# One more round between the attention and the MLP transposes of the first layer, on every engine

## The chip, the cores and the metric

The kernel runs on one core of one Trainium2 chip, as one launch. The metric is the device time of that core in microseconds (us). A core has five engines that run their own instruction lists in order and meet only at semaphores: PE (TensorE, matmuls and transposes), DVE (VectorE), ACT (ScalarE), POOL (GpSimd) and SP (SyncE, which issues the DMAs). An instruction whose semaphore is not there yet holds up everything behind it on its own engine.

## The reference

The model has four layers of attention and feed-forward on `x` of 16 x 256 x 128 floats. Each half layer is `x = x + layernorm(f(layernorm(x)))`. The change touches the first layer only:

```
def _L0_attn_ref(inputs, Wq, Wk, Wvdown, Wvup):
    Q = inputs @ Wq
    K = inputs @ Wk
    score = jnp.einsum('bqd,bkd->bqk', Q, K) / jnp.sqrt(jnp.float32(D))
    score = jnp.where(causal, score, 0.0)
    score = jnp.where(score != 0, score, NEG_FILL)
    attn = jax.nn.softmax(score, axis=-1)
    V = inputs @ (Wvdown @ Wvup)
    return attn @ V
x = x + _layernorm(_L0_attn_ref(_layernorm(x, axis=-1), ...), axis=-1)
x = x + _layernorm(_L0_ffn_ref(_layernorm(x, axis=-1), ...), axis=-1)
```

`_L0_ffn_ref` is a gated MLP with 384 hidden columns: `silu(x @ wg.T) * (x @ wu.T)`, and then the product with the down weights. The second layer (`L1`) has local and linear attention with an MLP, four times over.

## The kernel before

**Lanes and rounds.** The 4096 rows of `x` are eight groups of 512, each a tile of 128 x 4 x 128. The first phase (`phase1`) takes each group through the first layer (`pe_l0`, `dve_l0`, `act_l0`, `pool_l0`) and the four blocks of the second (`pe_l1` and so on). Four lanes, 0 to 3, take two groups one after the other: lane 0 groups 0 and 4, lane 1 groups 1 and 5. Each engine's list is written by the same scheme: for each lane a generator, and `together` (L140) asks each live lane once a round, lane 0 first, for what it issues up to its next `yield`. A lane joins at the round that `START1 = (0, 4, 9, 13)` (L21) gives. Rounds exist only in the order of the lists; no clock and no barrier belongs to them. A `yield` with nothing ahead of it issues nothing: it moves all that follows in this lane behind the next round of the other lanes.

**The 13 rounds of the first layer.** On PE, step 0 is empty; 1 transposes of the attention input (`pe_tr4`, L289); 2 q, k and v (L667, L668, L672); 3 scores (L681); 4 transposes of the probabilities (L690); 5 probabilities times v (L701); 6 empty; 7 transposes of the MLP input (L289 again); 8 to 10 gate and up (L714, L716), one hidden tile a round; 11 down (L723); 12 empty. A block of the second layer has 17 rounds, the fourth 18. In its order stand transposes (step 2), q and k (3; L743, L744), the values with the first `pe_by_query` (4; L750, L584, L587, L371), the second `pe_by_query` (5), the transposes of the maxima (6; L613), and later `pe_mlp` (L315 up, L324 down).

**What lies between steps 5 and 7.** DVE scales the attention output (L893), takes the statistics (L239, L242), POOL takes the power -1/2 (L276), DVE normalises (L251), adds to `x` (L283), takes the statistics again and negates the mean (L258); POOL takes the power and the product for the shift (L276, L270); ACT normalises in four instructions (`act_norm`, L263), and only then can PE transpose. ACT copies the transposed tile out of PSUM (L297) for step 8.

**What else orders the work.** Lanes 0 and 2 share PSUM banks 4 and 5, lanes 1 and 3 banks 6 and 7 (`lanes1`), and all share banks 0 to 3 for scores and `pe_by_query`. `Banks.fill` makes PE wait, before it fills a bank, for whoever reads what was filled in it last. In step 3 of the first layer DVE masks the scores in eight instructions (L880 to L886), ACT takes the exponentials (L982); silu is L998, the gelu of the second layer's MLP L334. A change among exp, silu and gelu on ACT costs an ACT_TABLE_LOAD.

The phases behind the first (`sync_all(..., "p1")`) begin when all engines are done with it, and the change does not touch them.

Of the kernel before, what the change touches and what calls it, by code (L numbers as in the profile page):

```python
# [160 lines left out]
def build(nc, tables, wa, wb, wc, wd, wm, wi, ve, co, step, frame, xin, out):  # L161
    ctx = ExitStack()
    with ctx:
# [175 lines left out]
        def idle(n):  # L339
            for _ in range(n):  # L340
                yield
# [314 lines left out]
        def pe_l0(pe, c, g):  # L656
            v = views01(c)
            XN, XT, QT, KT = v["XN"], v["XT"], v["QT"], v["KT"]
            k = (g, "l0a")
            yield  # L660
            pe.wait_ge(c.A, (k, "normed", 3))
            pe_tr4(pe, c, k, XN, 0, c.A)
            yield
            pe.wait_dma(got_wa0)
            ps, p2 = c.bank(pe, 0, c.D, (k, "q")), c.bank(pe, 1, c.A, (k, "k"))
            pe.wait_ge(c.A, (k, "xT"))
            pe.e.matmul(ps[0:32, :], wv("wq0"), XT, start=True, stop=True).then_inc(*c.P.inc((k, "q_pe")))  # L667
            pe.e.matmul(p2[0:32, :], wv("wk0"), XT, start=True, stop=True).then_inc(*c.P.inc((k, "k_pe")))  # L668
            pe.wait_ge(AD[LANES], "wv")
            c.banks.fill(pe, 3, c.A, (k, "v"))  # L670
            for t in range(4):
                ins = pe.e.matmul(psum[3][:, t * 128:(t + 1) * 128], XT[:, t * 128:(t + 1) * 128], WV, start=True, stop=True)  # L672
            ins.then_inc(*c.P.inc((k, "v_pe")))
            yield
            pe.wait_ge(c.D, (k, "q"))
            pe.wait_ge(c.A, (k, "k"))
            for b in range(2):
                for n in range(2):
                    t = 2 * b + 1 - n
                    c.banks.fill(pe, 2 * b + n, c.D, (k, b, "masked"))  # L680
                    ins = pe.e.matmul(psum[2 * b + n][:, 0:256], QT[0:32, t * 128:(t + 1) * 128],  # L681
                                      KT[0:32, b * 256:(b + 1) * 256], start=True, stop=True)
                ins.then_inc(*c.P.inc((k, b, "scores")))
            yield
            for b in range(2):
                for n in range(2):
                    c.banks.fill(pe, 2 * b + n, c.A, (k, b, "pT"))
                    pe.wait_ge(c.A, (k, b, n, "exp"))
                    for j in range(2):
                        ins = pe.e.transpose(psum[2 * b + n][:, j * 128:(j + 1) * 128],  # L690
                                             v["sc"][:, b, n, j * 128:(j + 1) * 128], ident)
                ins.then_inc(*c.P.inc((k, b, "tr")))
            yield
            ps = c.bank(pe, 0, c.D, (k, "o"))
            pe.wait_ge(c.A, (k, "v"))
            for b in range(2):
                pe.wait_ge(c.A, (k, b, "pT"))
                for n in (1, 0):
                    t = 2 * b + 1 - n
                    for j in range(2):  # L700
                        ins = pe.e.matmul(ps[:, t * 128:(t + 1) * 128], v["sT"][:, b, n, j * 128:(j + 1) * 128],  # L701
                                          v["V0"][:, 2 * b + j, :], start=j == 0, stop=j == 1)
            ins.then_inc(*c.P.inc((k, "av")))
            yield
            k = (g, "l0f")
            yield
            pe.wait_ge(c.A, (k, "normed", 3))
            pe_tr4(pe, c, k, XN, 0, c.A)
            yield
            pe.wait_ge(DD[LANES], "wgu")  # L710
            for j in range(3):
                ps, p2 = c.bank(pe, 0, c.A, (k, "h", j)), c.bank(pe, 1, c.D, (k, "hu", j))
                pe.wait_ge(c.A, (k, "xT"))
                pe.e.matmul(ps[:, :], WGU[:, j * 128:(j + 1) * 128], XT, start=True, stop=True).then_inc(  # L714
                    *c.P.inc((k, "gate", j)))
                pe.e.matmul(p2[:, :], WGU[:, 384 + j * 128:384 + (j + 1) * 128], XT, start=True, stop=True).then_inc(  # L716
                    *c.P.inc((k, "up", j)))
                yield
            ps = c.bank(pe, 0, c.A, (k, "y"))
            pe.wait_ge(c.D, (k, "hu", 2))  # L720
            for t in range(4):
                for j in range(3):
                    ins = pe.e.matmul(ps[:, t * 128:(t + 1) * 128], v["h3"][:, j, t * 128:(t + 1) * 128], wgd[:, j, :],  # L723
                                      start=j == 0, stop=j == 2)
            ins.then_inc(*c.P.inc((k, "sum")))
            yield
            yield
# [134 lines left out]
        def dve_l0(dve, c, g):  # L862
            v = views01(c)
            X, XN, O4, Z, VQ = XG[g], v["XN"], v["O4"], v["Z"], v["VQ"]
            k = (g, "l0a")
            dve.wait_dma(got_x[g])
            dve_stats(dve, c, k, X)
            yield
            yield
            dve.wait_ge(c.P, (k, "q_pe"))  # L870
            dve.e.tensor_scalar(v["QT"][0:32, :], c.ps[0][0:32, :], float(32.0 ** -0.5), None, ALU.mult).then_inc(
                *c.D.inc((k, "q")))
            yield
            dve.wait_dma(got_step)
            st, step2 = v["st"], bass.AP(tensor=STEPM.tensor, offset=STEPM.offset, ap=[STEPM.ap[0], [128, 2], [1, 256]])
            for b in range(2):
                src = PS[:, 1024 * b:1024 * b + 1024].rearrange("p (n c) -> p n c", c=512)[:, :, 0:256]
                sc, zz = v["sc"][:, b, :, :], v["zz"][:, b, :, :]
                dve.wait_ge(c.P, (k, b, "scores"))
                dve.e.tensor_tensor(sc, src, step2, ALU.mult).then_inc(*c.D.inc((k, b, "masked")))  # L880
                dve.wait_ge(c.D)
                dve.e.tensor_scalar(zz, sc, 0.0, FMIN, ALU.is_equal, ALU.mult).then_inc(*c.D.inc())
                dve.wait_ge(c.D)
                dve.e.tensor_tensor(sc, sc, zz, ALU.add).then_inc(*c.D.inc())
                dve.wait_ge(c.D)
                dve.e.tensor_reduce(st[:, 2 * b:2 * b + 2], sc, X_AX, ALU.max, negate=True).then_inc(*c.D.inc((k, b, "max")))  # L886
            yield
            yield
            dve.wait_ge(c.A, (k, 1, 0, "exp"))
            dve.e.reciprocal(st[:, 8:12], st[:, 4:8]).then_inc(*c.D.inc())  # L890
            dve.wait_ge(c.D)
            dve.wait_ge(c.P, (k, "av"))
            dve.e.tensor_tensor(O4, v4(c.ps[0]), st[:, 8:12].unsqueeze(2).to_broadcast([128, 4, 128]), ALU.mult).then_inc(  # L893
                *c.D.inc((k, "o")))
            yield from dve_post(dve, c, (g, "l0ap"), X, O4)
            k = (g, "l0f")
            dve_stats(dve, c, k, X)
            yield
            yield
            for j in range(3):  # L900
                dve.wait_ge(c.A, (k, "h", j))
                dve.wait_ge(c.P, (k, "up", j))
                dve.e.tensor_tensor(v["h3"][:, j, :], v["h3"][:, j, :], c.ps[1][:, :], ALU.mult).then_inc(
                    *c.D.inc((k, "hu", j)))
                yield
            dve.wait_ge(c.A, (k, "y"))
            yield from dve_post(dve, c, (g, "l0fp"), X, O4)
            yield from dve_norm(dve, c, (g, "z"), X, Z)
            dve.e.memset(VQ[:, :, 64:65], 1.0).then_inc(*c.D.inc((g, "ones")))
# [56 lines left out]
        def act_l0(act, c, g):  # L966
# [24 lines left out]
            k = (g, "l0f")  # L991
            yield
            act_norm(act, c, k, XG[g], v["XN"])
            act_copy(act, c, k, XT, c.ps[0][:, :], "tr", "xT")
            yield
            for j in range(3):
# [58 lines left out]
        def pool_l0(pool, c, g):  # L1055
            v = views01(c)
            yield from pool_norm_shift(pool, c, (g, "l0a"))
            yield from idle(4)
            yield from pool_norm(pool, c, (g, "l0ap"))
            yield from pool_norm_shift(pool, c, (g, "l0f"))  # L1060
            yield from idle(4)
            yield from pool_norm(pool, c, (g, "l0fp"))
            yield from pool_norm(pool, c, (g, "z"))
            pool.e.memset(v["VH"], 0.0).then_inc(*c.G.inc())
            pool.wait_ge(c.G)
            pool.e.memset(v["VP"][:, :, :, 16:17], 1.0)
            pool.e.memset(v["LT"][:, :, 0:64], 0.0)
            pool.e.memset(v["CP"], 0.0).then_inc(*c.G.inc((g // 4, "zeros", c.n)))
# [1720 lines left out]
```

## Time and profile before

| what | value |
|---|---|
| median of the runs | 3525.3 us (3525.18, 3525.3, 3534.24) |
| profiled execution | 3526.35 us |
| its span, first to last instruction | 3524.3 us |
| mean granted TensorE clock | 0.902 of full speed |
| busy over the span | PE 82%, DVE 64%, ACT 53%, POOL 14% |
| chain that ended last, by engine | PE 53%, DVE 32%, ACT 11%, issue 3%, POOL 1% |

The median is 1.05 us under the profiled execution, and the latter 2.05 us over its own span. The chain of the last row is followed back from the last instruction: at each step to what released it, or to the instruction before it on its engine. A busy PE may run at either of two clocks, 1.2 and 2.4 GHz, shown as a granted clock of 0.5 or 1.

### The profile page before, as it was taken

What the parts mean: (1) busy time and instruction counts of PE and PEld (TensorE: products, weight loads), DVE (VectorE), ACT (ScalarE), POOL (GpSimd) and SP (SyncE); (2) the same over time, 40 slices, a digit from 0 to 9 for tenths busy, and PEclk for the clock granted to TensorE, in tenths of its full rate; (3) what the DMA queues carried; (4) which work ended last, traced back from release to release, by engine and by line L of the source; (5) the groups of instructions that cost most, each with busy time, mean ns of one, the idle gap of its engine ahead of it and who ended that gap; (6) DMA issues with size and microseconds to landing.
All of it is one profiled execution on the core that took longest, in us unless ns stands there. A gap on an engine that the chain in (4) does not pass through costs nothing.

```text
span 3524.3 us, 76318 instructions
## 1 busy us (share of the span) xinstructions
PE 2884.4 (82%) x32152; PEld 2313.3 (66%) x32152; DVE 2249.2 (64%) x5958; ACT 1858.5 (53%) x4138; POOL 477.0 (14%) x543
## 2 busy tenths in 40 slices
PE   5788887788888667888885879997888899787895
PEld 3566665556666467777775667876767688675474
DVE  4665556675656489888887755457575644764527
ACT  3566665466666477777774444344544434444232
POOL 1110101210010132222221101120010211002000
PEclk8899998899999789888998799997989999797897
DMA  2000000000000100000000000010010000101000
GB/s 93 1 1 2 1 1 1 1 1 2 1 1 2 52 5 9 7 7 7 7 1 23 39 3 25 1 49 2 3 49 3 25 1 14 37 3 49 0 1 25
DMA packets 16998, 48.98 MB, mean 14 GB/s; under 512 B 1168, under 2 KB 9616, under 8 KB 14096
## 3 DMA queue, kind: packets, MB, share of 16 engines
q1 hardware_dynamic: 16656, 44.10, 3.6%
q8 instruction: 254, 4.16, 0.5%
q14 instruction: 88, 0.72, 0.1%
HBM read 41.99 MB, written 2.10 MB: 13 GB/s over the span
## 4 chain that ended last, share of the span: by engine, by line
PE 53%; DVE 32%; ACT 11%; issue 3%; POOL 1%; DMA 0%; DVEq 0%; SPq 0%; POOLq 0%; ACTq 0%
PE ps L324 7%; DVE LN L2012 5%; PE ps L315 4%; PE ps L1890 3%; PE ps L1352 3%; PE ps L381 3%; PE ps L468 3%; DVE M L484 2%; DVE LN L2025 2%; PE ps L1363 2%; PE ps L289 2%; DVE RS L239 2%; ACT LN L263 2%; ACT LN L297 2%; PE ps L1834 2%
## 5 line engine op out<-in xcount | busy, mean ns | idle before, releaser
L297 ACT COPY LN<-ps 128x512 f32<-128x512 f32 (+5 forms) x592 | 300.8, 547 | 316.4 <-PE ps L289 65.0
L276 POOL TENSOR_TENSOR RS<-RS,MISC 128x4 f32<-128x4 f32 x184 | 188.7, 1025 | 1509.6 <-DVE RS L258 800.2
L484 DVE TENSOR_REDUCE M<-ps 128x6 f32<-128x768 f32 x256 | 241.4, 954 | 131.9 <-PE ps L468 93.7
L289 PE MATMUL ps<-cons,LN 128*128 128x128 f32 x672 | 127.8, 329 | 183.7 <-ACT LN L263 90.6
L289 PEld LDWEIGHTS ps<-cons,LN 128*128 128x128 f32 x672 | 91.1, 167 | 227.0 <-ACT LN L263 84.6
L2012 DVE TENSOR_TENSOR LN<-LN 128x1024 f32<-128x1024 f32 (+2 forms) x192 | 220.3, 1147 | 27.8 <-ACT LN L297 16.2
L381 PE MATMUL ps<-LN 32*128 32x256 f32 x1024 | 188.6, 443 | 54.2 <-DVE LN L520 31.6
L629 DVE TENSOR_REDUCE M<-ps 128x12 f32<-128x1536 f32 x64 | 112.4, 1756 | 180.2 <-PE ps L371 180.2
L315 PE MATMUL ps<-LN,wAB 128*128 128x512 f32 x384 | 201.1, 656 | 15.3 <-DVE LN L952 15.3
L1890 PE MATMUL ps<-LN,wAB 128*128 128x128 f32 x1024 | 152.4, 312 | 74.2 <-ACT LN L297 73.7
L384 PE MATMUL ps<-LN 32*128 32x256 f32 x1024 | 203.6, 477 | 3.3 <-DVE M L484 3.3
L1936 ACT ACTIVATE LN<-LN,RS 128x128 f32<-128x128 f32 x512 | 198.7, 400 | 1.6 <-DVE RS L2037 0.6
L324 PE MATMUL ps<-wAB,LN 128*128 128x128 f32 x1536 | 189.4, 284 | 8.7 <-DVE LN L1511 5.2
L1890 PEld LDWEIGHTS ps<-LN,wAB 128*128 128x128 f32 x1024 | 145.1, 226 | 78.1 <-ACT LN L297 77.2
L324 PEld LDWEIGHTS ps<-wAB,LN 128*128 128x128 f32 x1536 | 183.1, 199 | 18.9 <-DVE LN L1511 9.1
L2095 POOL TENSOR_TENSOR LN<-LN,M 128x2048 f32<-128x2048 f32 x32 | 146.3, 4572 | 357.2 <-DVE M L2044 357.2
L544 ACT ACTIVATE LN<-ps 128x768 f32<-128x768 f32 x128 | 103.7, 810 | 170.0 <-PE ps L468 133.9
L534 ACT ACTIVATE LN<-ps 128x768 f32<-128x768 f32 x128 | 103.8, 811 | 113.0 <-PE ps L371 94.1
L1834 PE MATMUL ps<-wAB,LN 128*128 128x128 f32 x1024 | 125.7, 281 | 24.2 <-ACT LN L297 22.9
L263 ACT ACTIVATE LN<-LN,RS 128x128 f32<-128x128 f32 x256 | 104.9, 488 | 75.3 <-POOL RS L270 74.3
L381 PEld LDWEIGHTS ps<-LN 32*128 32x128 f32 x1024 | 83.2, 192 | 90.9 <-issue 38.8
L2064 DVE SCALAR_TENSOR_TENSOR LN<-LN,RS,ps 128x128 f32<-128x128 f32 x448 | 119.3, 339 | 35.0 <-PE ps L1890 34.9
(363 smaller groups left out, 7459.5 us busy)
## 6 DMA issues: line engine op xcount, KB each, us to landing
LN<-frame SPq DMA_DIRECT2D x16, 1024.0 KB, 4.8
wAB<-wb SPq DMA_DIRECT2D x16, 256.0 KB, 2.6
LN<-frame SPq DMA_DIRECT2D x8, 512.0 KB, 3.6
LN<-wd SPq DMA_DIRECT2D x8, 512.0 KB, 7.0
wAB<-wa SPq DMA_DIRECT2D x1, 3840.0 KB, 16.6
wCs<-wc SPq DMA_DIRECT2D x1, 2336.0 KB, 11.1
XA<-xin SPq DMA_DIRECT2D x8, 256.0 KB, 7.7
y<-XA SPq DMA_DIRECT2D x8, 256.0 KB, 2.3
```

The source lines that it names most:

```text
L276: pool.e.tensor_tensor(c.r[:, 40:44], c.r[:, 36:40], mhalf, ALU.pow).then_inc(*c.G.inc((k, "rstd")))
L289: ins = pe.e.transpose(ps[:, n * 128:(n + 1) * 128], src[:, n, :], ident)
L297: act.e.copy(dst, ps).then_inc(*c.A.inc(named(k, done)))
L315: pe.e.matmul(ps[:, :], w1[:, j * 128:(j + 1) * 128], xT, start=True, stop=True).then_inc(*c.P.inc((k, "up", j)))
L324: ins = pe.e.matmul(ps[:, t * 128:(t + 1) * 128], h3[:, j, t * 128:(t + 1) * 128], w2[:, j, :], start=j == 0, stop=j == nh - 1)
L381: pe.e.matmul(psum[n][:, 0:256], qt.ka[rows[j], o:o + 128], qt.qa[rows[j], o:o + 256], start=True, stop=False)
L384: pe.e.matmul(psum[n][:, 128:384], qs.qa[rows[j], o + 128:o + 256], qs.ka[rows[j], o:o + 256], start=True, stop=False)
L484: return dve.e.tensor_reduce(cols[:, 2 - 2 * h:4 - 2 * h, :, q.at], src, X_AX, ALU.max, negate=True)
L1834: ins = pe.e.matmul(psum[4 + g][:, i * 128:(i + 1) * 128], XTA[:, t * 128:(t + 1) * 128], phi[:, q * 128:(q + 1) * 128], start=True, stop= ...
L1890: ins = pe.e.matmul(psum[2 * gp + n][:, i * 128:(i + 1) * 128], eTb[2 * gp + n][:, i * 128:(i + 1) * 128], v["ym"][:, 4 * g + i, :], start ...
L1936: ins = act.e.activation(v["L3"][:, b, :], v["L3"][:, b, :], ACT.Exp, bias=v["nm"][:, b:b + 1], accum_out=v["rs"][:, b:b + 1])
L2012: dve.e.tensor_tensor(dst, src[:, 0:n, :], src[:, n:2 * n, :], op).then_inc(*c.D.inc())
```

## The change

`pe_l0` gets an empty round ahead of the MLP transposes, `dve_l0` one ahead of the first product with the gate, `act_l0` one between `act_norm` and the copy of the transposed tile, and `pool_l0` idles five rounds in place of four. So the first layer takes 14 rounds on each engine: the norm of ACT stays in step 7, the transposes come in step 8, gate and up in 9 to 11, down in 12, and all that follows in a lane comes one round later (two in its second group). The rounds at which lanes start stay.

```
@@ pe_l0
             k = (g, "l0f")
             yield
+            yield
             pe.wait_ge(c.A, (k, "normed", 3))
             pe_tr4(pe, c, k, XN, 0, c.A)
@@ dve_l0
             dve_stats(dve, c, k, X)
             yield
             yield
+            yield
             for j in range(3):
@@ act_l0
             act_norm(act, c, k, XG[g], v["XN"])
+            yield
             act_copy(act, c, k, XT, c.ps[0][:, :], "tr", "xT")
@@ pool_l0
             yield from pool_norm_shift(pool, c, (g, "l0f"))
-            yield from idle(4)
+            yield from idle(5)
             yield from pool_norm(pool, c, (g, "l0fp"))
```

No instruction is added or taken out but one ACT_TABLE_LOAD, of which there is one more after. Once two lanes have both passed the added round, they stand to each other as before. So the order differs only from the first layer's step 7 of lane 0 to that of lane 3, once for each group: rounds 7 to 20 in the first group (now 7 to 21), and the like in the second. Behind the added round the kernel's line numbers after are higher by 1 to 3.

On PE at the start of the program, the first place: lane 1's q, k and v, then lane 0's MLP transposes (L289) before, ahead of lane 1's scores (L681).

```order
L667 MATMUL ps<-LN,wAB 32x512
L668 MATMUL ps<-LN,wAB 32x512
L672 MATMUL ps<-wCs,LN 128x128 x4
L289 MATMUL ps<-cons,LN 128x128 x4
L681 MATMUL ps<-LN 128x256 x4
L714 MATMUL ps<-LN,wCs 128x512
L716 MATMUL ps<-LN,wCs 128x512
L690 MATMUL ps<-cons,LN 128x128 x8
```

The same place on PE after:

```order
L667 MATMUL ps<-LN,wAB 32x512
L668 MATMUL ps<-LN,wAB 32x512
L672 MATMUL ps<-wCs,LN 128x128 x4
L681 MATMUL ps<-LN 128x256 x4
L289 MATMUL ps<-cons,LN 128x128 x4
L690 MATMUL ps<-cons,LN 128x128 x8
L715 MATMUL ps<-LN,wCs 128x512
L717 MATMUL ps<-LN,wCs 128x512
```

Lane 1's scores now stand ahead of lane 0's transposes, and lane 1's transposed probabilities (L690) ahead of lane 0's first gate and up.

On ACT in the second group, the second place, before: lane 0's norm (L263) and copy (L297), lane 1's exponentials, lane 2's gelu (L334), lane 0's silu (L998).

```order
L263 ACTIVATE LN<-XA,RS 128x128 [waits pool_done0]
L263 ACTIVATE LN<-XA,RS 128x128 x3
L297 COPY LN<-ps 128x512 [waits pe_done0]
L982 ACT_TABLE_LOAD
L982 ACTIVATE LN<-LN 128x256 [waits dve_done1]
L982 ACTIVATE LN<-LN 128x256
L982 ACTIVATE LN<-LN 128x256 [waits dve_done1]
L982 ACTIVATE LN<-LN 128x256
L334 ACT_TABLE_LOAD
L334 ACTIVATE LN<-ps,vecs 128x512 [waits pe_done2] x2
L998 ACT_TABLE_LOAD
L998 ACTIVATE LN<-ps 128x512 [waits pe_done0]
```

The same place on ACT after:

```order
L263 ACTIVATE LN<-XA,RS 128x128 [waits pool_done0]
L263 ACTIVATE LN<-XA,RS 128x128 x3
L984 ACT_TABLE_LOAD
L984 ACTIVATE LN<-LN 128x256 [waits dve_done1]
L984 ACTIVATE LN<-LN 128x256
L984 ACTIVATE LN<-LN 128x256 [waits dve_done1]
L984 ACTIVATE LN<-LN 128x256
L334 ACT_TABLE_LOAD
L334 ACTIVATE LN<-ps,vecs 128x512 [waits pe_done2] x2
L297 COPY LN<-ps 128x512 [waits pe_done0]
L990 COPY LN<-ps 128x512 [waits pe_done1] x2
```

The copy of lane 0's transposed tile now comes behind lane 1's exponentials and lane 2's gelu.

On PE in the second group, the third place, before: lane 3's q, k, v, lane 0's q and k of the second layer (L743, L744), lane 2's MLP transposes (L289), lane 3's scores (L681), and lane 0's values and first `pe_by_query`.

```order
L672 MATMUL ps<-wCs,LN 128x128 x4
L743 MATMUL ps<-LN,wAB 128x512
L744 MATMUL ps<-LN,wAB 128x512
L289 MATMUL ps<-cons,LN 128x128 x4
L681 MATMUL ps<-LN 128x256 x4
L750 MATMUL ps<-wAB,LN 128x256 x4
L584 MATMUL ps<-LN 128x256 x4
```

The same place on PE after; the first L289 is lane 0's, of the second layer, the second lane 2's MLP transposes:

```order
L672 MATMUL ps<-wCs,LN 128x128 x4
L289 MATMUL ps<-cons,LN 128x128 x4
L724 MATMUL ps<-wCs,LN 128x128 x12
L681 MATMUL ps<-LN 128x256 x4
L744 MATMUL ps<-LN,wAB 128x512
L745 MATMUL ps<-LN,wAB 128x512
L289 MATMUL ps<-cons,LN 128x128 x4
L690 MATMUL ps<-cons,LN 128x128 x8
L751 MATMUL ps<-wAB,LN 128x256 x4
L584 MATMUL ps<-LN 128x256 x4
```

Lane 3's scores now stand ahead of lane 0's q and k, and lane 3's transposed probabilities follow two short steps behind them.

## Rows read from the trace of the kernel before

**Rows 1.** Four stretches: length, busy us per engine, granted clock, DMA share, GB/s.

```profile
10.00:168.00 158.00, 111.89 (x672) 71.72 (x672) 95.07 (x340) 71.33 (x149) 28.50 (x44) 0.83 0.09 35
594.00:752.00 158.00, 120.57 (x824) 81.91 (x824) 103.77 (x378) 83.70 (x160) 32.90 (x48) 0.88 0.00 1
168.00:594.00 426.00, 363.59 (x4168) 281.39 (x4168) 254.66 (x735) 268.43 (x477) 42.16 (x65) 0.94 0.01 1
752.00:1190.00 438.00, 374.04 (x4284) 289.92 (x4285) 260.80 (x758) 273.53 (x480) 44.74 (x67) 0.94 0.01 1
```

**Rows 2.** Waits, first 1200 us: total us, times, longest.

```profile
PE ps L289 <- ACT LN L263: 52.9, 16, 6.8
```

**Rows 3.** Timeline of PE, 30 to 72 us: start, us, instruction, idle before and releaser.

```profile
37.31 1.16 PE L672 MATMUL ps<-wCs,LN 128*128 128x128 f32 x8
43.65 1.11 PE L289 MATMUL ps<-cons,LN 128*128 128x128 f32 x4 [5.18 <-ACT LN L263]
44.69 3.78 PE L681 MATMUL ps<-LN 32*128 32x256 f32 x8
...
59.28 1.95 PE L701 MATMUL ps<-LN 128*128 128x128 f32 x16
...
67.97 1.12 PE L289 MATMUL ps<-cons,LN 128*128 128x128 f32 x4 [5.02 <-ACT LN L263]
```

**Rows 4.** Timeline of PE, 72 to 146 us.

```profile
76.38 1.12 PE L289 MATMUL ps<-cons,LN 128*128 128x128 f32 x4 [2.22 <-ACT LN L263]
...
83.17 1.99 PE L681 MATMUL ps<-LN 32*128 32x256 f32 x8
...
88.74 0.63 PE L690 MATMUL ps<-cons,LN 128*128 128x128 f32 x4 [1.67 <-ACT LN L982]
91.24 1.09 PE L690 MATMUL ps<-cons,LN 128*128 128x128 f32 x4 [1.87 <-ACT LN L982]
...
112.07 0.66 PE L289 MATMUL ps<-cons,LN 128*128 128x128 f32 x4 [3.40 <-ACT LN L263]
...
125.32 0.72 PE L584 MATMUL ps<-LN 32*128 32x256 f32 x8 [0.82 <-ACT LN L988]
...
143.58 0.66 PE L289 MATMUL ps<-cons,LN 128*128 128x128 f32 x4 [3.42 <-ACT LN L263]
```

**Rows 5.** Timeline of PE, 611 to 730 us, the second group.

```profile
614.65 0.66 PE L289 MATMUL ps<-cons,LN 128*128 128x128 f32 x4 [2.11 <-ACT LN L263]
615.23 3.48 PE L681 MATMUL ps<-LN 32*128 32x256 f32 x8
...
626.00 1.10 PE L714 MATMUL ps<-LN,wCs 128*128 128x512 f32 x2 [1.74 <-ACT LN L334]
...
645.50 1.12 PE L289 MATMUL ps<-cons,LN 128*128 128x128 f32 x4 [5.26 <-ACT LN L263]
...
654.83 0.66 PE L289 MATMUL ps<-cons,LN 128*128 128x128 f32 x4 [2.22 <-ACT LN L263]
...
694.80 1.11 PE L289 MATMUL ps<-cons,LN 128*128 128x128 f32 x4 [3.39 <-ACT LN L263]
695.85 3.78 PE L681 MATMUL ps<-LN 32*128 32x256 f32 x8
...
727.44 0.66 PE L289 MATMUL ps<-cons,LN 128*128 128x128 f32 x4 [3.42 <-ACT LN L263]
```

**Rows 6.** Timeline of DVE, 30 to 146 us.

```profile
40.47 0.67 DVE L871 TENSOR_SCALAR LN<-ps 32x512 f32<-32x512 f32 x1
...
113.82 0.69 DVE L880 TENSOR_TENSOR LN<-ps,wCs 128x512 f32<-128x512 f32 x1 [0.40 <-PE ps L681]
...
118.52 0.69 DVE L886 TENSOR_REDUCE LN<-LN 128x2 f32<-128x512 f32 x1
```

**Rows 7.** Timeline of ACT, 594 to 640 us.

```profile
623.30 1.28 ACT L334 ACT_TABLE_LOAD   x1
624.59 1.26 ACT L334 ACTIVATE LN<-ps,vecs 128x512 f32<-128x512 f32 x2
```

More of the change, by code:

```diff
@@ L706, in pe_l0 @@
             yield
+            yield
             pe.wait_ge(c.A, (k, "normed", 3))
@@ L899, in dve_l0 @@
             yield
+            yield
             for j in range(3):
@@ L993, in act_l0 @@
             act_norm(act, c, k, XG[g], v["XN"])
+            yield
             act_copy(act, c, k, XT, c.ps[0][:, :], "tr", "xT")
@@ L1060, in pool_l0 @@
             yield from pool_norm_shift(pool, c, (g, "l0f"))
-            yield from idle(4)
+            yield from idle(5)
             yield from pool_norm(pool, c, (g, "l0fp"))
```

## The prediction

> **What bounds the kernel now.** I read the busy time by stretches first, then the waits of PE in the first phase, then the timeline of PE where the order changes, and last DVE and ACT beside it. The stretches are to show that the two passages through the first layer are the loose part of the phase: PE is busy 111.89 of 158 us and 120.57 of 158 us there (71 and 76%), at a granted clock of 0.83 and 0.88, against 363.59 of 426 and 374.04 of 438 (85%) at 0.94 between and behind them [rows 1]. No other engine fills these passages either: DVE, the next, is busy 95.07 and 103.77 us. So they are set by waits from engine to engine in an in-order list, and PE's work alone is not the bound. The list of waits is to show which: PE stood 52.9 us, 16 times, at transposes for ACT's norm [rows 2]. That total holds the transposes of both halves of the layer; the change speaks only to those of the MLP, eight times: 5.18, 2.22, 3.40, 3.42 in the first group [rows 3, 4] and 2.11, 2.22, 3.39, 3.42 in the second [rows 5], together 25.36 us. The two longest (5.02 and 5.26 us at 67.97 and 645.50) are at lane 2's attention transposes, which the change doesn't move away from their norm [rows 3, 5].
>
> **What is removed and moved.** Nothing that costs time is removed. Each of the eight waits has other lanes' work pushed ahead of it, at least one step (2 to 6 us), so I count all eight as gone as they stand. What decides is what PE meets in place of them. I walked the new order of PE through both passages, with durations of the rows, and compare at three points that have the same work behind them up to one gate-and-up step. A gate-and-up step is set at 2.0 us, as two such instruction pairs take at the higher clock, the 1.10 us of 626.00 being the first pair [rows 5].
>
> *Lane 0's transposes to lane 2's attention transposes.* First group: PE ends lane 1's values at 38.47 (37.31 + 1.16) and would go to lane 1's scores. They need lane 1's q, which DVE copies until 41.14 (40.47 + 0.67) [rows 3, 6]. So 2.7 us of the 5.18 stay, and scores start at 41.2 in place of 44.69: 3.5 us earlier. Masks and exponentials follow from the scores alone, and with lane 0's transposes (1.1 us) as the only cover lane 1's L690 waits for them, about 3 us, so that the gain stays a matter of the chain. The product with v, 59.28 before, follows near 54 to 56, and lane 2's transposes, which hang on it through DVE (67.97 - 59.28 = 8.7 us), near 63.6: 4.4 us earlier, but with lane 0's third gate-and-up step (2.0) still owed. Second group: the 2.11 and 1.74 go, but lane 0's transposes now need bank 4, filled just ahead by lane 2's MLP and read by its gelu. On ACT that gelu stands behind lane 1's exponentials and a table load. The gelu pair began at 624.59, 9.4 us after the scores began at 615.23 [rows 5, 7]; with the scores at 612.6 it begins near 621.6, so PE, done with the scores, lane 2's up and lane 3's step near 618.3, waits about 4 us. Lane 2's transposes come near 642.6 in place of 645.50: 2.9 us earlier, 2.0 owed.
>
> *Lane 2's to lane 3's attention transposes.* The work is the same on both sides. Lane 1's MLP wait goes (2.22, both times). In place of it: lane 2's q meets bank 5 right behind lane 0's gate-and-up step, whose reader DVE waits for silu (0.8 and 1.8 us); lane 2's L690 has one step ahead of it in place of two. From the start of the scores to the second L690 it was 91.24 - 83.17 = 8.1 us; cover is now 2.0 + 1.9, so with the first half taken out (0.6) some 3 us stand in place of 1.67 + 1.87 [rows 4]. I set -2.0 for the first group, 0 for the second.
>
> *Lane 3's attention transposes to lane 2's MLP transposes and lane 3's scores.* Lane 2's wait (3.40, 3.39) should go and does not: its bank 4 was filled by lane 0's q, which DVE copies (L924) behind lane 3's masks, since lane 3's scores now come ahead of lane 0's q. The masks take 118.52 + 0.69 - 113.82 = 5.4 us [rows 6], and cover is q, k (2.0): 3.0 to 3.3 us. The releaser changes, the wait stays. The owed gate-and-up step is paid here: +2.2 in the first group, +0.5 in the second.
>
> *To lane 3's MLP transposes.* The 3.42 goes. Waits for lane 3's copy go too, the 0.82 of 125.32 [rows 4] being one of a few under 1 us. New are lane 0's transposes of the maxima right behind one gate step, and `pe_by_key` behind lane 2's statistics on DVE, about 2.0 us each. -2.0 in each group, and once both lanes are past, the old order returns.
>
> Sum, first group: -4.4 - 2.0 + 2.2 - 2.0 = -6.2; second: -2.9 + 0 + 0.5 - 2.0 = -4.4. Together -10.6, of 25.4 on offer: the rest turns into waits on banks and on DVE's queue. The unknown is the clock. Lane 1's scores took 3.78 us at 44.69, lane 2's 1.99 at 83.17, lane 3's 3.78 at 695.85 behind the 3.39 wait [rows 3 to 5]: the lower and the higher clock (1.2 and 2.4 GHz). A scores step that moves from behind a wait gives back 1.8 us, and one that falls behind a new one costs as much. From below, no such gain (0); from above, lane 0's and lane 3's scores-like steps in each group (4 x 1.8 = 7.2), and losses of the same size. I take -0.4, since old and new waits are near each other in number. Total -11, on 3526.35: 3515.3, and 1.05 less for the median: 3514.
>
> POOL's idle round moves with the others and issues nothing. The rest of POOL, SP and all DMAs are not moved past anything: their share in the passages is 0.09 and 0.00 [rows 1], and nothing waits for them. The one more ACT_TABLE_LOAD, 1.28 us [rows 7], is on an engine busy 71.33 of 158 us [rows 1]; it counts only inside the chains above, in which I have it. Uncovered it costs 1.3.
>
> The activation behind the load starts at 624.59, that is 0.01 us after 623.30 + 1.28 [rows 7]. The Trainium skill, page ScalarE: Activation LUTs, section "What ACT_TABLE_LOAD costs", counts a drain of about 1.38 us on top of each load, 2.66 in all. By that rule lane 0's transposes in the second group would wait 1.4 us longer and the total be -9.6; the row shows no such gap, so it isn't counted.
>
> **The rivals.** *All of it is gained.* The chains I let stand behind the moved steps shorten as well, and the clock stays high. For: eight stops ended by one releaser, in passages with 24 to 29% of PE idle. Against: bank 4 and DVE's queue are named in the new order. It gives 3526.35 - 25.4 - 1.05 = 3500, or some us less with the clock. The granted clock goes to half after stops, as the 3.78 behind 3.39 shows; by the Trainium skill, page TensorE: Matmul & The Clock Gate, section "Part 1", activity releases the throttle and idleness brings it back, so fewer stops should pay twice. The trace agrees at 695.85.
>
> *Nothing is gained.* The engines behind the stops, DVE above all, set the pace: lane 2's attention transposes hang 8.7 us behind the product with v in either order, and the two new waits on DVE and bank 4 (3.0 to 4.0 us, three times) with the new ones at the maxima take the other half. 10.6 less the 11 of these being somewhat longer: 3520 to 3530, 3525 as its value.
>
> *Slower: the rounds set the pace.* Two rounds more are issued. In the 426 us from lane 0's 24th to its 86th round a round took 426 / 62 = 6.9 us [rows 1]. If a lane's step in the passages waits for its own step of the round before, and the others for the lane ahead through banks, an added round costs a round: 2 x 6.9 = 13.7 us, and 3539. For: bank 4 and 5 tie lane 0 to lane 2 and 6 and 7 lane 1 to lane 3; against: in rounds 6 and 7 lane 0 has nothing to issue and the other lanes fill them. It decides from the point where new waits sum to over 25.4 us, 3.2 for each one removed. If the change did nothing, the order on PE would be the old one; it isn't.
>
> **How the numbers follow.** Forecast 0.50 (its own range 3507 to 3520), all gained 0.13, nothing gained 0.22, slower 0.15. A measurement of this kernel can tell about 0.3%, 10.6 us, from no change: faster means under 3514.7. Of the forecast 0.30 lies there and 0.20 within; of "nothing", 0.17 within and 0.05 slower. So faster 0.43, same 0.37, slower 0.20. The range 3499 to 3533 leaves out half of the slower rival and little of the first.
>
> **What would show it.** In the profile after, PE's wait at L289 for L263 over the first 1200 us should fall from 52.9 by about 20 to 25 us, to 28 to 33 and 8 to 9 times. Lane 0's MLP transposes in the second group should wait near 4 us for L334, lane 2's 3 us for DVE L924 (L926 after), lane 2's q for a DVE product. The first phase should end 11 us earlier, and the 426 us between the passages should stand unchanged within 3. I am wrong if that stretch changes, if a stop at lane 3's L690 or at the maxima exceeds 5 us, or if phases behind the first differ by more than 3 us.

## The result and the profile after

The changed kernel takes 3512.95 us in the median of 13 runs, the kernel before 3531.55 in 13 runs beside it; the ratio is 0.9955, 95% interval 0.9944 to 0.9965, some 16 us faster (the two medians lie 18.6 us apart). On another occasion the ratio was 0.9947 (0.9927 to 0.9967). The profiled execution takes 3512.27 us with a span of 3510.2, 14.1 under the span before. The forecast was 3514, the range 3499 to 3533. (The kernel before ran between 3523 and 3550 us over all runs of this study, so ratios are used below and not times.)

First the totals of PE's waits after, for the first 1186 us, which end at the same step as the 1200 us of [rows 2]:

```profile
PE ps L289 <- ACT LN L263: 25.5, 8, 6.4
```

52.9 us in 16 waits became 25.5 in 8: the fall is 27.4. The eight MLP waits make 25.4 of it. Another 1.6 is lane 3's attention transposes in the second group, which stopped for 2.51 us before and stop for 0.88 after (669.11 below); 0.4 is the first wait of the program.

```profile
680.61 1.97 PE L289 MATMUL ps<-cons,LN 128*128 128x128 f32 x8 [2.51 <-ACT LN L263]
```

(Over the first 1200 us of the changed kernel as they stand, the line is 38.2 in 11, since a wait of 10.1 us that stands behind the first phase in both kernels has moved into them.) What came in their place is in the timeline of PE after, in the first group (start, us, instruction, idle before and releaser). The lines answer to [rows 3, 4]:

```profile
37.70 1.16 PE L672 MATMUL ps<-wCs,LN 128*128 128x128 f32 x8
41.79 3.78 PE L681 MATMUL ps<-LN 32*128 32x256 f32 x8 [2.94 <-DVE LN L872]
45.50 1.11 PE L289 MATMUL ps<-cons,LN 128*128 128x128 f32 x4
...
63.61 1.12 PE L289 MATMUL ps<-cons,LN 128*128 128x128 f32 x4 [5.01 <-ACT LN L263]
...
75.56 0.60 PE L289 MATMUL ps<-cons,LN 128*128 128x128 f32 x4
76.09 1.99 PE L681 MATMUL ps<-LN 32*128 32x256 f32 x8
...
91.60 0.60 PE L289 MATMUL ps<-cons,LN 128*128 128x128 f32 x4
...
110.21 1.08 PE L289 MATMUL ps<-cons,LN 128*128 128x128 f32 x4 [3.92 <-DVE LN L926]
...
125.08 0.41 PE L613 MATMUL ps<-cons,M 128*128 128x128 f32 x2 [2.11 <-DVE M L633]
...
129.58 0.71 PE L599 MATMUL ps<-LN 32*128 32x256 f32 x8 [1.93 <-DVE LN L640]
...
138.67 0.60 PE L289 MATMUL ps<-cons,LN 128*128 128x128 f32 x4
```

The MLP transposes at 45.50, 75.56 and 138.67 (lanes 0, 1, 3) have no wait any more. Lane 2's, at 110.21, wait 3.92 us for DVE's copy of lane 0's q, where 3.40 had stood for the norm. The second group, to be held against [rows 5]:

```profile
605.17 1.99 PE L681 MATMUL ps<-LN 32*128 32x256 f32 x8
...
614.71 0.74 PE L289 MATMUL ps<-cons,LN 128*128 128x128 f32 x4 [3.85 <-ACT LN L334]
...
634.53 1.12 PE L289 MATMUL ps<-cons,LN 128*128 128x128 f32 x4 [5.25 <-ACT LN L263]
...
649.75 0.60 PE L289 MATMUL ps<-cons,LN 128*128 128x128 f32 x4
...
669.11 0.66 PE L289 MATMUL ps<-cons,LN 128*128 128x128 f32 x4 [0.88 <-ACT LN L263]
...
687.77 1.09 PE L289 MATMUL ps<-cons,LN 128*128 128x128 f32 x4 [3.92 <-DVE LN L926]
...
716.37 0.60 PE L289 MATMUL ps<-cons,LN 128*128 128x128 f32 x4
```

The MLP transposes are those at 614.71, 649.75, 687.77 and 716.37 (lanes 0 to 3); lanes 1 and 3 have no wait.

Last, PE's busy time between the same steps of both kernels: the first passage (from lane 1's v to the transposed maxima at 196.77 before, 189.62 after), the stretch between the passages, and the second passage (from lane 1's q). The columns are those of [rows 1]. Before:

```profile
37.31:196.77 159.46, 118.31 (x862) 79.88 (x861) 105.08 (x369) 79.33 (x157) 31.35 (x49) 0.83 0.00 1
196.77:567.39 370.62, 318.83 (x3759) 246.27 (x3759) 218.88 (x617) 238.92 (x423) 34.78 (x53) 0.95 0.01 2
604.99:780.54 175.55, 135.46 (x981) 93.56 (x981) 117.75 (x419) 93.71 (x176) 35.41 (x53) 0.87 0.00 1
```

After:

```profile
37.70:189.62 151.92, 114.68 (x861) 77.87 (x860) 103.80 (x369) 78.84 (x157) 30.73 (x50) 0.84 0.00 1
189.62:560.10 370.48, 318.90 (x3759) 246.42 (x3759) 218.87 (x617) 238.90 (x423) 34.78 (x53) 0.95 0.01 2
597.69:767.25 169.56, 129.54 (x981) 90.19 (x981) 117.20 (x419) 94.38 (x177) 34.73 (x53) 0.90 0.00 1
```

The passages are 7.54 and 5.99 us shorter, 13.5 of the 14.1; the stretch between them is the same to 0.14 us. The same matmuls kept PE busy 3.63 and 5.92 us less, at a granted clock of 0.84 and 0.90 in place of 0.83 and 0.87; PE's idle time fell by 3.91 and 0.07. So 27.4 us of waits for the norm went, and PE's idle time fell by 4.0 in all: the rest became other waits. The phases behind the first, which the change doesn't touch, took 2378.6 us, counted from the last transposed maxima of the first phase to the end, against 2380.0 before.

### The profile page after: what moved, and what is told of

Read it like the earlier page. It is cut to its first block, busy times and chain, and to the rows that moved or that the text cites. A ratio compares the mean times of both kernels' runs of the same rounds, so it can differ in the third digit from the quotient of the medians.

```text
span 3510.2 us, 76317 instructions
## 1 busy us (share of the span) xinstructions
PE 2872.7 (82%) x32152; PEld 2306.8 (66%) x32152; DVE 2247.4 (64%) x5958; ACT 1858.8 (53%) x4139; POOL 475.5 (14%) x543
## 4 chain that ended last, share of the span: by engine, by line
PE 54%; DVE 33%; ACT 10%; issue 3%; POOL 1%; DMA 0%; DVEq 0%; SPq 0%; POOLq 0%; ACTq 0%
PE ps L324 7%; DVE LN L2015 5%; PE ps L315 4%; PE ps L1893 3%; PE ps L1355 3%; PE ps L381 3%; PE ps L468 3%; DVE M L484 2%; DVE LN L2028 2%; PE ps L1366 2%; DVE RS L239 2%; PE ps L289 2%; ACT LN L297 2%; PE ps L1837 2%; DVE M L629 1%
## 5 line engine op out<-in xcount | busy, mean ns | idle before, releaser
L297 ACT COPY LN<-ps 128x512 f32<-128x512 f32 (+4 forms) x592 | 300.3, 546 | 304.1 <-PE ps L289 57.5
L289 PE MATMUL ps<-cons,LN 128*128 128x128 f32 x672 | 126.2, 326 | 166.4 <-ACT LN L263 63.2
L289 PEld LDWEIGHTS ps<-cons,LN 128*128 128x128 f32 x672 | 90.4, 165 | 208.8 <-ACT LN L263 53.5
L263 ACT ACTIVATE LN<-LN,RS 128x128 f32<-128x128 f32 x256 | 104.8, 488 | 78.5 <-POOL RS L270 77.5
```

Source lines behind the costliest of these rows:

```text
L289: ins = pe.e.transpose(ps[:, n * 128:(n + 1) * 128], src[:, n, :], ident)
L297: act.e.copy(dst, ps).then_inc(*c.A.inc(named(k, done)))
```

## The experiments

All ratios are to the kernel before, from runs beside it on the same chip. Diffs are to the changed kernel where nothing else is said, shown on PE where the other engines have the like.

**One group at a time.**

```
             yield
-            yield
+            if g < 4:          # e2: g >= 4
+                yield
```

> The added round only in the first group of each lane. Place theory (the gain is that of the MLP transposes standing one round further from their norm, passage by passage): the profile of the changed kernel runs 7.15 us ahead of the kernel before between the two passages, so this kernel is 7 us faster than before (ratio 0.998), and PE's wait for the norm at the transposes is about 45 us in the first 1200. Rival, the clock: the gain belongs to the whole phase and isn't split by passages; then 0 to 4 us or 10 us and more.

> The added round only in the second group of each lane. Place theory: 14.2 - 7.15 = 7 us faster than before (ratio 0.998), and the two single-group kernels add up to the whole change. Rival, that the second passage profits from the first one's shift: under 3 us here.

Measured: 0.9976 (0.9965 to 0.9987) for the first group alone, 0.9987 (0.9975 to 0.9999) for the second, about 8 and 5 us. Their product is 0.9963, within the intervals of the whole change. PE's wait for the norm over the first 1200 us of the first kernel is 39.3 us in 12, not the 45 expected. For the second kernel the interval runs from nothing to 9 us and doesn't exclude its rival; the traces say more. In the first kernel the first passage is 152.57 us long (159.46 before) and the second 175.54 (175.55 before). In the second kernel the second passage, from lane 1's q to the transposed maxima, is 167.90 us long. So each passage is shortened by its own round, by 6.9 and 7.7 us, as the place theory has it. In the first kernel PE's lead at the transposed maxima was 6.6 us behind the first passage and 6.8 at the end of the phase. In the second it *lagged* 10.2 us ahead of its passage, although its order there is that of the kernel before, and 3.4 behind it. 4.0 of the 10.2 were there at the end of the first passage; the rest is the stretch between the passages in that execution:

```profile
200.77:577.59 376.82, 328.95 (x3759) 253.02 (x3759) 218.90 (x617) 239.32 (x423) 34.79 (x53) 0.93 0.01 1
```

The 3759 matmuls are those of the 318.83 us before; here they took 328.95 at a clock of 0.93 and not 0.95, and the stretch 6.2 us more. Two more of the kernels below, with the same order in this stretch, took 374.6 and 374.9 us for it, and the others with this order 370.0 to 370.7. No kernel of this study was profiled on both sides; but the runs of the kernel before, beside these, lie between 3522.92 and 3541.14 us. So a single profile can't settle 5 us over the whole of this kernel.

**The round in another place.** Against the kernel before, on all engines:

```
             ins.then_inc(*c.P.inc((k, "sum")))
             yield
             yield
+            yield

         def pe_l1(pe, c, g, i):
```

> 14 rounds in the first layer, but the empty one stands at the end of the layer, so that the MLP transposes follow their norm as before. Place theory: the eight waits for the norm stay, about 25 us of them, and the time is that of before within 5 us. Rival, the round itself (any added round moves the lanes against each other and parts steps that meet at a bank): as fast as the change, 14 to 16 us faster. Rival, rounds set the pace: 2 x 6.9 = 13.7 us slower.

Measured: 1.0004 (0.9993 to 1.0014). PE's total for L263 in the first 1215 us of this kernel was 66.6 us in 17 waits, one of 10.1 us among them that stands behind the first phase in every kernel. Without it that is 56.5 in 16, against 52.9 in 16 before. With 14 rounds, but not in this place, nothing is gained. The added round as such costs little either: by the interval at most 5 us, not the 13.7 of the slower rival.

**The norm moved along.**

```
             k = (g, "l0f")
             yield
+            yield
             act_norm(act, c, k, XG[g], v["XN"])
-            yield
             act_copy(act, c, k, XT, c.ps[0][:, :], "tr", "xT")
```

> As the change, but on ACT the norm itself also comes one round later, in the round of the transposes, behind the other lanes' exponentials; PE, DVE and POOL are those of the change. Place theory: the distance from norm to transposes on ACT's list decides, so PE waits for the norm again, and 0 to 6 us of the gain are left. Rival (PE's round alone, more work of PE ahead of the transposes, is the whole of it): 14 to 16 us faster than before.

Measured: 1.0047 (1.0029 to 1.0065), 16 us *slower* than before and some 32 slower than the change, from four norm instructions a group that stand one round later on ACT. Both theories missed even the sign. The two passages are 165.68 and 185.34 us long, 6.2 and 9.8 more than before. The timeline of PE shows lane 0's transposes, first and second group:

```profile
49.62 1.11 PE L289 MATMUL ps<-cons,LN 128*128 128x128 f32 x4 [6.15 <-ACT LN L263]
```
```profile
631.70 1.11 PE L289 MATMUL ps<-cons,LN 128*128 128x128 f32 x4 [5.87 <-ACT LN L263]
```

They waited 5.18 and 2.11 for the norm before [rows 3, 5] and 0 and 3.85 after, the latter for a gelu. The norm now stands behind lane 1's exponentials, which wait for DVE's masks, as ACT's timeline of the first group shows:

```profile
44.44 0.51 ACT L984 ACTIVATE LN<-LN 128x256 f32<-128x256 f32 x1 [7.17 <-DVE LN L887]
...
46.94 0.51 ACT L984 ACTIVATE LN<-LN 128x256 f32<-128x256 f32 x1 [1.41 <-DVE LN L887]
...
47.94 1.63 ACT L263 ACTIVATE LN<-XA,RS 128x128 f32<-128x128 f32 x4
```

PE's waits for the norm in the first phase are 61.8 us in 16, against 52.9 before and 25.5 in the changed kernel. So the change needs both: PE's transposes later and ACT's norm where it was.

**A second round in the same place**, on all engines:

```
             k = (g, "l0f")
             yield
             yield
+            yield
             pe.wait_ge(c.A, (k, "normed", 3))
```

> A second empty round behind the first, 15 rounds in the first layer. Place theory: hardly a wait for the MLP norm is left to save (none of the eight in the changed kernel's first 1200 us), so the second round buys nothing: ratio to the kernel before 0.994 to 0.998. Rival, rounds set the pace: the second round costs 2 x 6.9 = 13.7 us against the changed kernel, ratio 0.999 to 1.000. Rival, distance goes on paying: another 10 us and more, ratio under 0.993.

Measured: 0.9935 (0.9912 to 0.9958). The interval overlaps that of the change; whether the second round gains something is open. In the profiled execution it is 5.9 us ahead of the changed kernel at the last transposed maxima of the first phase (1125.67 against 1131.60) and 0.9 behind it at the end. The part in between, which is the same in all kernels here, took from 2375.7 to 2386.8 us in the profiled executions of this study, so this lead neither shows a gain nor excludes one. It does not cost 13.7 us, which is the second time that the slower rival fails.

**A round at the attention's norm too.**

```
             k = (g, "l0a")
             yield
+            yield
             pe.wait_ge(c.A, (k, "normed", 3))
```
```
             act_norm(act, c, k, XG[g], v["XN"])
+            yield
             act_copy(act, c, k, XT, c.ps[0][:, :], "tr", "xT")
```

> The change, and a like empty round between the norm and the transposes of the attention input, in every lane, 15 rounds. In the changed kernel PE still stops 5.01 and 5.25 us for the norm at lane 2's attention transposes. Place theory: these go, about half comes back as other waits, 2 to 7 us faster than the change (ratio to the kernel before 0.9935 to 0.995). Rival, the chain from the product with v through DVE is the bound there and not the order on PE: no gain, ratio 0.995 to 0.997; rounds set the pace: 0.999 to 1.000.

> The changed kernel once more, beside the others on the same chip: ratio to the kernel before 0.9945 to 0.9965.

> The kernel with a round at both norms once more, beside the change on the same chip: 3 to 9 us faster than the change, ratio to the kernel before 0.992 to 0.994.

Measured: 0.9909 (0.9887 to 0.9932), and at the second time, beside the change, 0.9912 (0.9891 to 0.9933) against the change's 0.9947 (0.9927 to 0.9967): medians 3503.63 and 3513.8 us. That is the expected direction and more than the expected size. The two intervals of the second time overlap, but its four runs (3501.14 to 3506.95) all lie below the six of the change beside them (3508.28 to 3525.06). The stops of 5.01 and 5.25 us at lane 2's attention transposes are gone. PE's waits for the norm in the first 1215 us:

```profile
PE ps L289 <- ACT LN L263: 29.4, 13, 10.1
```

In the changed kernel it is 44.1 in 16 over the same 1215 us; of the first phase alone it is 25.5 in 8 there and 10.9 in 5 here. This version is faster than both kernels. Its variant with a second MLP round:

> One round at the attention's norm and two at the MLP's, 16 rounds. The second MLP round gained 0 to 7 us on the change by itself in the lead over the kernel before at the first passage (13.2 against 7.2 us) and lost it again elsewhere. Place theory: the same as the two-norm kernel, ratio 0.990 to 0.994. Rounds set the pace: 5 us and more slower than that one.

Measured: 0.9906 (0.9888 to 0.9924), median 3501.66. It cannot be told from the one with 15 rounds, as expected.

**Lane 2's round at the attention's norm instead.**

```
             k = (g, "l0f")
             yield
-            yield
+            if not (c.n == 2):
+                yield
```

and `if c.n == 2: yield` ahead of the attention's transposes, with the like on the other engines.

> As the change in lanes 0, 1 and 3; lane 2 gets its one added round at the attention's norm instead of the MLP's, so that all lanes still have 14 rounds and the second layer's order is that of the change. Lane 2's MLP transposes waited 3.92 us in the changed kernel too, for a bank and not for the norm, so nothing is lost there, and the 5.01 and 5.25 us at its attention transposes should go: 4 to 9 us faster than the change, ratio to the kernel before 0.993 to 0.9945. Rival, DVE's chain is the bound there: as the change, 0.995 to 0.9965, with the wait found one step further on.

Measured: 0.9976 (0.9963 to 0.999), about 7 us slower than the change by the ratios (it wasn't run beside it; the medians lie 14 us apart) where 4 to 9 faster was expected. The place theory fell; the rival's 0.995 to 0.9965 just touches the interval. PE's timeline in the first group, at lane 2's MLP transposes:

```profile
115.67 1.11 PE L289 MATMUL ps<-cons,LN 128*128 128x128 f32 x4 [9.68 <-ACT LN L263]
```

And ACT's ahead of it:

```profile
112.92 0.49 ACT L992 ACTIVATE LN<-LN 128x256 f32<-128x256 f32 x1
113.32 0.19 ACT L992 ACTIVATION_READ_ACCUMULATOR LN<-LN 128x1 f32 x1
113.41 0.67 ACT L1025 ACTIVATE LN<-ps,cons 128x512 f32<-128x512 f32 x1
113.98 1.64 ACT L263 ACTIVATE LN<-XA,RS 128x128 f32<-128x128 f32 x4
```

The 5.01 us at lane 2's attention transposes went, but lane 3's, which had none in the first group of the changed kernel, now stop for 3.23 us. And lane 2's MLP norm fell one round back and stands behind lane 3's exponentials, as lane 0's in the kernel with the late norm. DVE's copy that frees the bank of these transposes is later too; first here, then in the changed kernel:

```profile
112.29 0.68 DVE L932 TENSOR_SCALAR LN<-ps 128x512 f32<-128x512 f32 x1
```
```profile
109.38 0.68 DVE L926 TENSOR_SCALAR LN<-ps 128x512 f32<-128x512 f32 x1
```

In the changed kernel lane 2's norm was done long before that copy:

```profile
102.97 1.65 ACT L263 ACTIVATE LN<-XA,RS 128x128 f32<-128x128 f32 x4
```

It ended at 104.62, 5.4 us ahead of the copy (110.06), and only because its round stood there. In this kernel the copy ends at 112.97 and the norm at 115.62: of the 9.68 us PE would have stood 7.0 for the copy, which is 2.9 us later than in the changed kernel, and 2.65 come on top for the norm. "Nothing is lost there" was read from the releaser's name, and that tells nothing of where the other condition will end once its own place in the list is changed.

**The stops filled, the order before kept.** Against the kernel before:

```
+            ps = c.bank(pe, 0, c.A, (k, "xT"))
+            for n in range(12):
+                pe.e.transpose(ps[:, 0:128], ident, ident)
             pe.wait_ge(c.A, (k, "normed", 3))
-            pe_tr4(pe, c, k, XN, 0, c.A)
+            for n in range(4):
+                ins = pe.e.transpose(ps[:, n * 128:(n + 1) * 128], XN[:, n, :], ident)
+            ins.then_inc(*c.P.inc((k, "tr")))
```

> The kernel before, order and all, but PE transposes the identity twelve times into the bank of the MLP transposes while it waits for their norm (1.9 us at the higher clock, 3.3 at the lower, overwritten after; eight such places). Clock theory: in the two profiles PE's busy time over the same instructions in the two passages fell by 9.6 of the 13.5 us that the change gained, so filling the stops alone gives part of it: 4 to 9 us faster than before, PE busy without the added transposes lower in the passages. Waits theory: the stops stay as long for the norm, so nothing is gained, or up to 5 us lost where the added work outlasts the stop.

Measured: 0.9987 (0.9976 to 0.9998): with 96 transposes more, it is some 5 us faster by the median ratio, with an interval from under 1 to 8 us. PE in the second group, to be held against [rows 5]:

```profile
617.18 1.53 PE L709 MATMUL ps<-cons 128*128 128x128 f32 x12
619.36 0.65 PE L712 MATMUL ps<-cons,LN 128*128 128x128 f32 x4 [0.65 <-ACT LN L263]
619.95 1.99 PE L681 MATMUL ps<-LN 32*128 32x256 f32 x8
...
630.07 1.86 PE L719 MATMUL ps<-LN,wCs 128*128 128x512 f32 x2 [4.43 <-ACT LN L334]
```

The scores behind the filled stop take 1.99 us and not 3.48: here the clock did stay up. In the first group, where 3.88 us of the stop are left behind the twelve transposes, it did not:

```profile
39.27 1.47 PE L709 MATMUL ps<-cons 128*128 128x128 f32 x12
44.62 1.11 PE L712 MATMUL ps<-cons,LN 128*128 128x128 f32 x4 [3.88 <-ACT LN L263]
45.67 3.78 PE L681 MATMUL ps<-LN 32*128 32x256 f32 x8
```

And in the second group the next stop, for ACT's gelu, grew from 1.74 to 4.43 us. From the start of the scores to this gate step it is 10.12 us here and was 10.77 before. The two passages as a whole, to be held against those before (159.46 and 175.55 us):

```profile
38.27:197.90 159.63, 123.48 (x909) 85.99 (x908) 104.72 (x369) 79.19 (x157) 31.66 (x49) 0.84 0.00 1
609.69:783.75 174.06, 130.61 (x1029) 91.86 (x1029) 117.57 (x419) 93.13 (x176) 35.58 (x53) 0.95 0.00 1
```

The added transposes are 6.00 and 6.06 us of the busy time. So in the second passage PE's own work took 124.6 us, 10.9 less than before and less than in the changed kernel (129.54), and yet the passage is only 1.5 us shorter; the first isn't shorter at all. This profile doesn't show where the 5 us of the medians come from. A higher clock on PE is a gain only as far as PE's work, and not a chain through DVE and ACT, leads to the next step.

## Why the prediction was right, and where it was not

*The number.* Eleven us of gain were forecast, from the 3525.3 that three runs of the kernel before had given; 16 were measured, against 3531.55 in 13 runs. That 3514 and 3512.95 lie so near each other is in part luck: the start was 6 us low and the gain 5 us short.

*The eight waits go.* Right: all eight are gone as waits for the norm. The line fell by 27.4 us, a little more than the 20 to 25 forecast, as two waits at attention transposes shrank with it. Of the 25.5 us that are left, 10.3 are the two stops named as not touched (5.01, 5.25); the largest of the others are 6.45 at the first transposes of the program and 4.76 at lane 0's attention transposes of its second group. (The total of 52.9 also held 1.17 and 1.71 us near the end of the phase, which belong to neither half of the first layer.) The kernel with the round at the end shows that it is this place and not the number of rounds.

*What PE meets instead.* Right by name and nearly by size: lane 1's scores for the q copy 2.94 (forecast 2.7), lane 0's second transposes for the gelu 3.85 (4), lane 2's for DVE's q copy 3.92 twice (3.0 to 3.3), the maxima 2.11 and `pe_by_key` 1.93 (2.0 each). Lane 2's q waits 0.94 and 1.75 us for a DVE product (0.8 and 1.8). None of the signs of being wrong came: the stretch between the passages stood, no stop at lane 3's L690 or at the maxima exceeded 5 us, and the phases behind the first differ by 1.4 us.

*The sum by checkpoints* (lead of the changed kernel, in us, from the rows above and [rows 3 to 5]):

| up to | first group, forecast | measured | second group, forecast | measured |
|---|---|---|---|---|
| lane 2's attention transposes | 4.4 | 67.97 - 63.61 = 4.4 | 2.9 | 645.50 - 634.53 - 7.3 = 3.7 |
| lane 3's attention transposes | +2.0 | +2.9 | 0 | +0.5 |
| lane 2's MLP transposes, lane 3's scores | -2.2 | -3.2 | -0.5 | -0.7 |
| lane 3's MLP transposes | +2.0 | +0.9 | +2.0 | +0.3 |
| together | 6.2 | 143.58 - 138.67 = 4.9 | 4.4 | 727.44 - 716.37 - 7.3 = 3.8 |

(7.3 is the lead with which the second passage begins, 604.99 - 597.69.) The last step was over-sized both times. Its waits fell by 1.7 and 1.5 us in sum, near the 2.0 forecast; but PE's own work took about 1 us more, since behind the two new stops (2.11 and 1.93 us) it ran slower. In the first group, before and after:

```profile
134.80 1.13 PE L743 MATMUL ps<-LN,wAB 128*128 128x512 f32 x2 [0.46 <-DVE LN L920]
135.76 1.02 PE L744 MATMUL ps<-LN,wAB 128*128 128x512 f32 x2
137.24 2.92 PE L723 MATMUL ps<-wCs,LN 128*128 128x128 f32 x24 [0.46 <-DVE LN L903]
```
```profile
131.28 2.07 PE L744 MATMUL ps<-LN,wAB 128*128 128x512 f32 x2 [0.56 <-DVE LN L922]
133.15 1.92 PE L745 MATMUL ps<-LN,wAB 128*128 128x512 f32 x2
134.86 3.98 PE L724 MATMUL ps<-wCs,LN 128*128 128x128 f32 x24
```

*What failed is "once both lanes are past, the old order returns", taken as the end of the account.* The order returns there, the clock does not yet: the lead grew from 4.9 to 7.15 us by the transposed maxima at 189.62, and from 3.8 to 6.0 at 767.25. The changed kernel comes to these steps without the 3.42 us stop ahead, and more of what follows runs at the higher clock. PE's waits between these steps did not fall (9.3 us before and after in the first group, 9.3 and 10.8 in the second), so the whole of it is PE's own work. That is 4.5 us more than forecast, against 1.9 less up to the checkpoints.

*The clock.* The term of -0.4 is the mis-sized one: PE's busy time over the passages fell by 9.55 us, and the passages by 13.5. A part of this was in the walk without being named, which used durations at the higher clock for scores and gate steps. The filled stops show that busy time saved isn't a passage shortened: 10.9 us less of PE's own work in the second passage, in the order before, made it 1.5 us shorter. How the 16 us split into clock and waits stays open; they aren't independent.

*The rivals.* "Slower, rounds set the pace" fell with the change itself and three times more: with the round at the end, with 15 and with 16 rounds. "All of it is gained" fell: 16 of 25.4, at most 20 by the interval. "Nothing is gained" fell by the interval.

## What to carry to other kernels

In a list-ordered kernel with in-order engines, a stop at a consumer was removed by moving the consumer one round back while its producer stays: moved together they cost 32 us here against the change, and an empty round elsewhere was worth nothing. Walk the new order by hand past the last changed place, up to where both traces are again at the same distance. The releaser of a wait is only the last to arrive. Before a step is given its round back because its wait has another name, look where the other conditions will end in the new order: lane 2's norm had ended 5.4 us ahead of the copy, and moved by one round it ended 2.65 behind (9.68 us of wait in place of 3.92). And a faster or busier PE is no gain by itself; only the passage's length counts.

## What the runs showed of the hardware

The same 3759 matmuls in the same order, between the same two steps, took 318.0 to 319.7 us of PE time in seven profiled executions (before, changed twice, first group alone, round at the end, two rounds, lane 2's round moved), and 325.0, 325.3 and 329.0 in three others (late norm, filled stops, second group alone). The mean granted clock was 0.95 to 0.96 in the seven and 0.93 in the three, and the stretch 370.0 to 370.7 us against 374.6, 374.9 and 376.8. What puts an execution on one side or the other isn't shown. In the kernel before PE idled 2.11 us and then ran lane 1's scores in 3.48 us, against 1.99 where twelve transposes had filled most of that wait; where 3.88 us of wait were left behind the twelve, the scores took 3.78. Behind ACT_TABLE_LOAD (1.28 us) the activation started within 0.02 us here too:

```profile
612.58 1.28 ACT L334 ACT_TABLE_LOAD   x1
613.88 1.26 ACT L334 ACTIVATE LN<-ps,vecs 128x512 f32<-128x512 f32 x2
```
